# Refilling a stacked key buffer per quad of heads instead of per stage, ahead of the output store in the SP queue

## What is computed

```python
def _L1_xattn_ref(x, cond, wq, bq, wkv, bkv, wp, bp):      # H = 16, Dh = 16
    q = _qdq(x) @ _qdq(wq).T + bq
    kv = cond @ wkv.T + bkv
    k, v = jnp.split(kv, 2, axis=-1)
    ...
    attn = jax.nn.softmax(jnp.einsum('bnhd,bmhd->bhnm', q, k) * scale, axis=-1)
    o = jnp.einsum('bhnm,bmhd->bnhd', attn, v).reshape(B, N, C)
    return _qdq(o) @ _qdq(wp).T + bp
...
x = x + _L1_xattn_ref(_layernorm(x, axis=-1), ctx_2048, ...)
x = x + _L1_ffn_ref(_layernorm(x, axis=-1), ...)
```

## Time and profile before

| | us |
|---|---|
| device time, median of 3 runs (lowest, highest) | 852.65 (852.61, 862.78) |
| span of the profiled execution | 856.0 |
| PE busy in it | 774.2 (90%) |
| DVE / ACT / POOL busy | 579.5 / 383.9 / 187.4 |
| mean granted TensorE clock, share of 2.4 GHz | 0.955 |
| reads of `kscr` into the stack (line 545) | 48 transfers of 400.2 KB |
| writes of `kscr` (line 540) | 24 transfers of 400.2 KB |

### The profile page before, as it was taken

How to read it: one execution, slowest core, us unless ns; L and a number is a source line. 1 busy time by engine, 2 the same in 40 slices (tenths; PEclk the granted TensorE clock), 3 DMA queues, 4 the chain that set the end, 5 groups by cost and what they waited for, 6 DMA issues and landing times.

```text
span 856.0 us, 12968 instructions
## 1 busy us (share of the span) xinstructions
PE 774.2 (90%) x5027; PEld 434.2 (51%) x5027; DVE 579.5 (68%) x1290; ACT 383.9 (45%) x563; POOL 187.4 (22%) x136
## 2 busy tenths in 40 slices
PE   6998999977999898889989899989899989889996
PEld 3534777744665565644434455534445544335434
DVE  4798767621857656777867687757687757857814
ACT  2100444344333323156746565546465546544680
POOL 2377323311902122200401304002104004000000
PEclk9899999999999999999989899999799999869999
DMA  9201100004499233450381650562640750830000
GB/s 305 103 0 30 49 1 1 1 2 175 97 150 134 72 37 56 53 87 2 85 89 53 137 63 2 118 69 77 122 54 1 131 55 2 140 34 1 14 1 13
DMA packets 31708, 55.94 MB, mean 65 GB/s; under 512 B 10804, under 2 KB 19764, under 8 KB 30741
## 3 DMA queue, kind: packets, MB, share of 16 engines
q1 hardware_dynamic: 31640, 55.03, 34.2%
HBM read 42.56 MB, written 12.46 MB: 64 GB/s over the span
## 4 chain that ended last, share of the span: by engine, by line
PE 52%; issue 15%; DMA 12%; DVE 11%; POOL 7%; SPq 2%; ACT 2%; POOLq 0%; DVEq 0%; ACTq 0%
DMA r<-kscr 10%; PE ps L963 8%; PE ps L1074 7%; PE ps L1053 5%; PE ps L851 5%; PE ps L783 3%; PE ps L820 3%; PE ps L927 3%; PE ps L907 2%; DVE small L1633 2%; PE ps L861 2%; PE ps L810 2%; POOL r L610 2%; DMA kscr<-r 2%; PE ps L739 1%
## 5 line engine op out<-in xcount | busy, mean ns | idle before, releaser
L1633 DVE TENSOR_REDUCE small<-ps 128x1 f32<-128x400 f32 (+1 forms) x512 | 286.4, 572 | 113.8 <-PE ps L963 108.0
L1444 ACT ACTIVATE r<-ps 128x1024 f32<-128x1024 f32 (+1 forms) x208 | 212.4, 1023 | 113.2 <-PE ps L1053 110.8
L963 PE MATMUL ps<-r 96*128 96x400 bf16 (+1 forms) x512 | 176.0, 351 | 29.4 <-DMA r<-kscr 15.8
L1074 PE MATMUL ps<-r 128*17 128x256 f32 (+1 forms) x1664 | 135.4, 399 | 2.2 <-ACT r L1444 2.0
L1053 PE MATMUL ps<-r 99*128 99x256 bf16 (+1 forms) x832 | 131.5, 282 | 0.0
L963 PEld LDWEIGHTS ps<-r 96*128 96x128 bf16 x512 | 50.2, 98 | 147.0 <-DVE small L1633 95.0
L1053 PEld LDWEIGHTS ps<-r 99*128 99x128 bf16 (+1 forms) x832 | 83.8, 102 | 34.0 <-issue 11.6
L628 POOL TENSOR_TENSOR r<-r 128x1601 bf16<-128x1601 f32 x8 | 26.0, 3254 | 222.2 <-ACT r L1285 222.2
L907 PE MATMUL ps<-r,hT 128*128 128x512 f32 (+1 forms) x160 | 67.5, 554 | 1.0 <-DVE r L1622 1.0
L851 PE MATMUL ps<-r,wkvT 128*128 128x400 f32 (+1 forms) x128 | 53.4, 516 | 6.4 <-issue 6.4
L861 PE MATMUL ps<-wkvT,r 128*128 128x256 f32 (+1 forms) x208 | 58.1, 398 | 0.0
(11 more groups left out here) (201 smaller groups left out, 1023.7 us busy)
## 6 DMA issues: line engine op xcount, KB each, us to landing
r<-kscr SPq DMA_DIRECT2D x48, 400.2 KB, 13.6
kscr<-r SPq DMA_DIRECT2D x24, 400.2 KB, 4.0
r<-in_ctx_dram SPq DMA_DIRECT2D x4, 1601.0 KB, 7.0
r<-qscr SPq DMA_DIRECT2D x24, 128.0 KB, 5.0
r<-in_wo_dram SPq DMA_DIRECT2D x1, 2048.0 KB, 12.0
r<-in_gu_dram SPq DMA_DIRECT2D x1, 2048.0 KB, 7.8
qscr<-qpart SPq DMA_DIRECT2D x24, 64.0 KB, 1.8
x<-in_x_dram SPq DMA_DIRECT2D x1, 1024.0 KB, 5.3
```

Of the source, the lines that this page charges most:

```text
L963: mm(bank(ca % 2)[:, 0:m], qst[0:SROWS, h, q0:q0 + P], kst[0:SROWS, s % 2, h % HALF, a:a + m], start=True, stop=True).then_inc(mx_mm, 1)
L1074: last = mm(bank(6)[32 * k:32 * k + VW, 0:LQ], vx[0:n, b % 2, kt, h, :], pr[i % 3][0:n, k * LQ:(k + 1) * LQ], start=kt == 0, stop=kt == KT ...
L1444: fn(pr[i % 3][0:n, :], bank(2 + 2 * (i % 2), 2)[0:n, :], ACT.Exp, scale=SCALE1)\
L1633: v.tensor_reduce(mxc[quad % 2][:, n:n + 1], bank(ca % 2)[:, 0:m], AX_X, ALU.max).then_inc(mx_rdy, 1)
```

## The change

`kst` and `kscr` stay as they are. The six reads of 8 heads become twelve of 4 heads: six for the first quad of the stage, then six for the second. Each quad has a semaphore of its own out of four (`k_stk[quad % 4]`); the first six wait for the scores of the quad 2s-4, the second six for those of the quad 2s-3 (`sc_mm >= KT * (quad - 3)`), which read just these heads of the half. The wait in front of the writes to `kscr` takes both quads' semaphores of stage s-2. PE's wait before the first maxima of a quad names that quad's semaphore. And in the loop over b, `stack_keys(2b+2)` now stands in front of `store(b-1)`.

```diff
-        k_stk = [sem(f"k_stk{i}") for i in range(2)]
+        k_stk = [sem(f"k_stk{i}") for i in range(4)]
...
                 if s >= 2:
-                    sp.wait_ge(k_stk[s % 2], 96 * (s // 2))
+                    for quad in (2 * s - 4, 2 * s - 3):
+                        sp.wait_ge(k_stk[quad % 4], 96 * (s // 2))
                 for j in range(3):
                     sp.dma_start(kscr[s % 2, j], kpart[s][j]).then_inc(k_wr, 16)
                 sp.wait_ge(k_wr, 48 * (s + 1))
-                if s >= 2:
-                    sp.wait_ge(sc_mm, 2 * KT * (s - 1))
-                for g, j in enumerate(STACK_K):
-                    sp.dma_start(kst[g * DH:(g + 1) * DH, s % 2], kscr[s % 2, j].rearrange("(h d) k -> d h k", d=DH))\
-                        .then_inc(k_stk[s % 2], 16)
+                for quad in (2 * s, 2 * s + 1):
+                    heads = slice(4 * (quad % 2), 4 * (quad % 2) + 4)
+                    if quad >= 4:
+                        sp.wait_ge(sc_mm, KT * (quad - 3))
+                    for g, j in enumerate(STACK_K):
+                        sp.dma_start(kst[g * DH:(g + 1) * DH, s % 2, heads],
+                                     kscr[s % 2, j].rearrange("(h d) k -> d h k", d=DH)[:, heads])\
+                            .then_inc(k_stk[quad % 4], 16)
...
             for b in range(B - 1):
+                stack_keys(2 * b + 2)
                 if b >= 1:
                     store(b - 1)
-                stack_keys(2 * b + 2)
...
                 if n == 0:
-                    pe.wait_ge(k_stk[s % 2], 96 * (s // 2 + 1))
+                    pe.wait_ge(k_stk[quad % 4], 96 * (quad // 4 + 1))
```

## The result

| | before | after |
|---|---|---|
| device time, median us (lowest, highest) | 853.95 (852.61, 862.78) | 830.98 (829.49, 838.13) |
| span of the profiled execution | 856.0 | 828.2 |
| PE busy | 774.2 (90%) | 763.1 (92%) |
| mean granted TensorE clock of the profiled execution | 0.955 | 0.973 |

The changed kernel takes 0.9719 times the kernel before (95% interval 0.9676 to 0.9762): 23.0 us less by the medians, 27.8 us less between the two profiled executions. The interval is wide: in microseconds it reaches from 20 to 28.

A forecast was written before the change was run, and what follows sets the result against it. PE, busy 90% of the span, was taken as the bound. Idle 15.85 us plus clock 11.0 us made 26.85 us, 856.0 to 829.15; the median 3.35 us lower, 825.8 us. Own range 819 to 833; top with rivals 838.

The forecast's parts named there:

- The four stalls: PE's waits on key-scratch reads at quads 4, 8, 12 and 14: 4.01, 4.15, 3.99, 3.70 us, all to vanish.
- Rival C: PE's wait moves to DVE's maxima and up to all the gain comes back: about 850 us, chance 0.05.
- The clock: Low-clock (1.2 GHz) stretches behind PE's four waits on the scratch vanish with them: 11.0 us gained.
- The first three terms: Low clock behind the waits at quads 4, 8 and 12: half the low time gained, 2.6 + 1.7 + 1.7 us.
- the last stretch: Low clock behind quad 14's wait, 756.80 to 769.00, 12.2 us: 5.0 us taken as gain, bounds 0 and 5.3.
- the three shift waits: PE's waits for the shift in the cross-attention, expected to stay; some 2 us of lost time allowed either way for each.
- The split: Twelve half-size reads per stage: stage 7's first quad there at 746.0, asked for at 753.1, margin 7 us, stall gone.
- The rate term: Refill reads at unchanged bytes per second: first six there after about 12.7 us, second six some 24 us after first issue.
- Rivals B and D: B: half-size reads cost as much as full ones, 836.5 us, chance 0.05. D: splitting hurts, 877 us, chance 0.02.
- The earlier permission: Stage 2's first six reads go at about 421 instead of 422.9; first quad there at about 434, margin 9 us.
- The store: Behind the refill in stages 4 and 6, leaving at about 546 instead of 540.8 in stage 4; cost zero.
- Rival E: PE's shift waits grow as POOL's subtractions hold DVE a second time in three stages: 840 us, chance 0.04.

The follow-up runs named there:

- dummy_work: Kernel before with 18 useless matmuls filling PE's idle stretch at quads 4, 8, 12 and 14: 851.0 us, ratio 0.9959 to before.
- order_only: Kernel before with the refill moved in front of the store, eight-head reads kept: 844.0 us, ratio 0.9901 to before.
- both_halves: Changed kernel, but a quad's first maxima wait for the semaphores of both quads of its stage: 840.02 us, ratio 0.9832 to before.
- same_partitions: Changed kernel with both half-size reads of a 16-partition group directly behind each other, all behind the late permission: 841.12 us in one run.
- split_only: Changed kernel with the output store back in front of the refill: 830.06 us, ratio 0.9748 to before.
- late_permission: Changed kernel, but a stage's first six reads wait for the scores of both quads of stage s-2: 830.54 us, ratio 0.9743 to before.
- two_heads: Changed kernel with 24 reads of two heads (100 KB) per stage instead of twelve of four: 830.7 us, ratio 0.9748 to before.

## Why the prediction was right

The forecast was 825.8 us, with 819 to 833 as its own range; 830.98 us were measured.

**The four stalls go, and nothing takes their place.** Right in all four places: 15.85 us of idleness less. Rival C did not occur: the maxima's waits on DVE are 5.6 us against 5.1.

**The clock.** Right in kind: the low stretches behind the stalls were the stalls' doing, as the windows after and dummy_work show. The size was off. The first three terms took half of the low time; with 0.40 to 0.45 us per us their 12.0 us come to 4.8 to 5.4 instead of 6.0. The 5.0 us for the last stretch were about what it cost in the profiled execution (5.5 us). But that execution was not typical. At the same place, behind waits of 4.82, 3.59 and 4.59 us, the clock was low from PE's resumption for 4.1 us in order_only, 5.8 in both_halves and 4.7 in same_partitions:

```profile
744.60:748.70 4.10, 4.06 (x24) 1.78 (x25) 1.75 (x3) 1.30 (x2) 0.00 (x0) 0.50 0.00 0
```

```profile
744.10:749.90 5.80, 5.78 (x36) 2.55 (x36) 3.29 (x7) 2.77 (x3) 0.00 (x0) 0.50 0.01 3
```

```profile
743.50:748.20 4.70, 4.70 (x27) 2.34 (x28) 2.25 (x5) 1.97 (x2) 0.00 (x0) 0.50 0.00 0
```

That is some 2 us in place of 5.0, and the sum 22.7 to 23.3 us instead of 26.85. It is an account made afterwards that fits the medians' 23.0; the interval of this one comparison, 20 to 28 us, would hold both sums. What speaks for the smaller gain is that split_only, late_permission and two_heads, which have no wait on the scratch either, came to ratios of 0.9743 to 0.9748. Against it stands the granted clock, whose median went from 0.960 to 0.974, some 25 us less at the lower level, 10 us at 0.4 rather than 7. That difference stays open.

That the profiled pair differs by 27.8 us, so near to 26.85, is in part luck. Behind the three shift waits, which the sum took as unchanged, the clock was low for 6.8, 10.2 and 6.8 us in the profiled execution of before and for 3.4, 10.2 and 3.4 us in that of after. That is worth some 3 us, with the waits themselves unchanged; it lies within the 2 us either way that I had allowed for each.

**From the span to the median.** I took the median to lie 3.35 us below the profiled span. In all runs since, the device time is 1.8 to 1.9 us above the span; so the profiled execution of before took about 857.8 us and was one with more low clock than most (0.955 against a median of 0.960 in the 13 executions of before beside the first experiments, some 9 us of low clock). Scaling one profiled execution to the median keeps what was peculiar to it in the sum: the forecast of 825.8 us lay 5.2 us below the measured median, while 829.15 was forecast for the span and 828.2 came.

**The split.** Right that it frees quad 14 with 7 us to spare (7.1 measured). The rate term was pessimistic: I assumed unchanged bytes per second, 12.7 and 24 us; it was 11.5 and 20.5 us. Rivals B and D would have needed half-size reads as dear as full ones or dearer. The Trainium skill's fixed part of about 2.0 us per DMA ("DMA: Bandwidth & Descriptors", section "Anatomy of one DMA", which speaks of DMAs issued by GpSimd; these are issued by SP) does not show as time added in this queue: 24 reads of a stage had a higher rate than six.

**The earlier permission.** I put stage 2's first reads at 421, with 4.05 us for the writes' landing, a figure of stage 7. They went at 422.93, as the writes landed, 6.4 us behind the first of them. The 6.0 us that SP waited for the scores of quad 1 ran for the most part while the writes were on their way anyway; about 1 us of it was the permission's. late_permission shows that the step buys nothing once each quad waits for its own four heads.

**The store.** Its move costs nothing, as said: it left at 538.68 with no one waiting. But it was not needed either: for the stalls of stages 4 and 6 the move and the split are each a sufficient remedy, and the split removes them with the store still in front.

**The shift waits** stayed three, of 2.61, 2.79 and 3.29 us, against 2.60, 2.80 and 3.30 before. Rival E did not occur.

## What to carry to other kernels

When an in-order engine waits for the last of a group of transfers, look which of them its next work needs, and give these a semaphore of their own. Here that was enough in all four places with the old order of the queue, and for stage 7 it was the only remedy found; in stages 4 and 6 an earlier start did as well. Two small changes that each remove the same wait don't add up, so test them apart before keeping both. And price a stall as its idle time plus a part for the clock, taken from several executions: one trace's longest low stretch is no basis.

## What the runs showed of the hardware

- Reads from DRAM into groups of 16 partitions, queued one behind the other, ran at 113 to 119 GB/s when 400 KB in a row went to one group, at 119 to 143 with 200 KB and at 135 to 148 with 100 KB. The DMA engines' share was 1.03 to 1.07 in all these windows, so a full share didn't mean that no more bytes could go through.
- Four idle stretches of 3.7 to 4.15 us were followed by 5.2, 3.4, 3.4 and 12.2 us at 1.2 GHz. How long it stays low varies: the same shift wait of 2.8 us was followed by 9.1 us of work at 1.2 GHz in the changed kernel and by none in split_only. Matmuls without use in the four stretches kept the clock up and more than paid for themselves (851.0 against 854.5 us, ratio 0.9959, 0.9924 to 0.9995).
- A microsecond of low clock cost 0.40 to 0.45 us here, not 0.5.
- DVE instructions with both inputs in SBUF were held to the end of a running POOL subtraction (1645 took 3.06 us instead of 0.17, 1730 2.98 instead of 0.68). A cast with a single input in SBUF was held as well: before the second and the third shift wait of the changed kernel 1647 took 3.08 us instead of 0.18. The reductions out of PSUM beside them kept their 0.56 to 0.6 us. Moving the last subtractions by two steps was worth 12 to 13 us, more than half as much as the change under study.
